# Narrow-head attention: steps of equal size, the first batch's split moved one phase ahead, one exponential for short units, loads and weights issued elsewhere

## What is computed

```python
x = x + _L0_attn_a(...)      # wide heads, not touched
x = x + _L0_ffn(...)         # experts, capacity routing
x = x + _L0_attn_b(...)      # narrow heads, cosine attention: |q| = |k| = 1, causal
x = x + _L0_ffn(...)
x = x + _L1_attn_a(...)      # narrow heads; query j of each 128 sees keys 0..j only
x = x + _L1_ffn(...)         # narrow heads, causal softmax; then 8 gated experts, top 2
x = x + _L1_attn_b(...)      # a recurrence (rwkv)
x = x + _L1_ffn(...)
# _L1_ffn, in short:
att = softmax(where(causal, q @ k.T / sqrt(8), -inf)); x = x + (att @ v) @ c_proj
h = gelu(x @ w1); y = h @ w2; x = x + sum of y of the two chosen experts, weighted
```

## Time and profile before

| | us |
|---|---|
| median of 3 runs | 2647.75 (2642.23 to 2649.84) |
| the profiled execution | 2645.61 |
| its span in the trace | 2643.7 |
| wide attention and first experts | 0 to 1051.6 |
| L0b: norms, attention | 1051.6 to 1071.6, 1072.3 to 1257.9 |
| window attention | 1435.8 to 1572.3 |
| L1 attention, first and second | 1600.4 to 1926.7, 2166 to 2493 |
| last gated experts | 2512.8 to 2643.7 |

### The profile page before, as it was taken

How to read it: one execution, slowest core, us unless ns; L and a number is a source line. 1 busy time by engine, 2 the same in 40 slices (tenths; PEclk the granted TensorE clock), 3 DMA queues, 4 the chain that set the end, 5 groups by cost and what they waited for, 6 DMA issues and landing times. The chain is left out here.

```text
span 2643.7 us, 37155 instructions
## 1 busy us (share of the span) xinstructions
PE 2140.0 (81%) x13716; PEld 1247.5 (47%) x13716; DVE 1591.2 (60%) x3477; ACT 1447.9 (55%) x2122; POOL 784.5 (30%) x428
## 2 busy tenths in 40 slices
PE   4999999999999538488346785999879737999798
PEld 3666666666666316122315342344347423444357
DVE  5978787787785465211564555777433666777324
ACT  3777777777777432598423243556653343555541
POOL 3877777687786002322003003000000031000000
PEclk7999999999999759699568796899989866999899
DMA  2000000000000310520501202211010012110010
GB/s 71 1 5 1 3 5 1 3 4 1 3 1 1 121 43 1 141 59 17 163 0 41 70 23 61 61 38 38 2 32 1 1 36 68 38 38 20 1 32 17
DMA packets 46411, 83.49 MB, mean 32 GB/s; under 512 B 11272, under 2 KB 19544, under 8 KB 43224
## 3 DMA queue, kind: packets, MB, share of 16 engines
q1 hardware_dynamic: 46232, 81.12, 11.2%
HBM read 64.09 MB, written 16.25 MB: 30 GB/s over the span
## 5 line engine op out<-in xcount | busy, mean ns | idle before, releaser
L713 ACT ACTIVATE probs<-psum_banks 128x1024 f32<-128x1024 f32 (+3 forms) x608 | 472.0, 827 | 357.3 <-PE psum_banks L581 258.6
L786 DVE TENSOR_REDUCE neg_max<-psum_banks 128x1 f32<-128x512 f32 (+3 forms) x672 | 398.5, 656 | 204.1 <-PE psum_banks L613 152.0
L1138 POOL TENSOR_SCALAR l0a_rows<-l0a_rows,l0a_rinv 128x1024 f32<-128x1024 f32 x160 | 454.4, 2845 | 188.8 <-DVE l0a_rinv L1100 185.1
L1088 DVE TENSOR_REDUCE l0a_nmax<-psum_banks 128x1 f32<-128x1024 f32 x256 | 312.4, 1220 | 137.7 <-PE psum_banks L982 135.7
L577 PE MATMUL psum_banks<-q_stack,k_stack 75*128 75x512 bf16 (+7 forms) x1216 | 295.6, 343 | 90.9 <-ACT probs L713 41.1
L1034 ACT ACTIVATE l0a_rows<-psum_banks,l0a_nmax 128x1024 f32<-128x1024 f32 x256 | 285.8, 1116 | 61.5 <-DVE l0a_nmax L1088 60.0
L609 PE MATMUL psum_banks<-k_stack,q_stack 72*128 72x128 bf16 (+3 forms) x1024 | 249.7, 327 | 79.3 <-DMA q_stack<-q_parts 67.2
L996 PE MATMUL psum_banks<-packed,l0a_rows 128*128 128x128 f32 x2048 | 266.2, 273 | 2.7 <-POOL l0a_rows L1138 1.6
L996 PEld LDWEIGHTS psum_banks<-packed,l0a_rows 128*128 128x128 f32 x2048 | 238.4, 141 | 42.9 <-issue 5.4
L981 PE MATMUL psum_banks<-l0a_kh,l0a_qw 128*128 128x512 f32 x512 | 241.1, 471 | 19.7 <-POOL l0a_qw L1127 13.5
L597 PE MATMUL psum_banks<-probs,v_ones 128*32 128x512 f32 (+3 forms) x2432 | 243.5, 515 | 7.7 <-ACT o_sum L682 6.5
(11 more groups left out here) (272 smaller groups left out, 3392.9 us busy)
## 6 DMA issues: line engine op xcount, KB each, us to landing
q_stack<-q_parts SPq DMA_DIRECT2D x72, 192.0 KB
k_stack<-k_parts SPq DMA_DIRECT2D x48, 192.0 KB
qkv<-in_l0f_w SPq DMA_DIRECT2D x6, 1024.0 KB, 5.5
q_parts<-parts SPq DMA_DIRECT2D x24, 256.0 KB, 3.3
k_parts<-parts SPq DMA_DIRECT2D x18, 256.0 KB, 4.9
moe_b<-in_l0f_b SPq DMA_DIRECT2D x32, 128.0 KB, 3.5
k_eight<-parts SPq DMA_DIRECT2D x16, 256.0 KB, 3.7
k_stack<-k_eight SPq DMA_DIRECT2D x16, 256.0 KB
```

What stands on the lines that cost most here:

```text
L713: act.activation(S.Pt[:, U % PBUFS, 2 * half:2 * half + 2, c0:HALF], PS[:, bank:bank + 2, c0:HALF], ACT.Exp).then_inc(exp_done, 1)
L786: dve.tensor_reduce(out, scores, AX, ALU.max, negate=True).then_inc(job_read, 1)
L1088: dve.tensor_reduce(R.nmax4[:, s % 4:s % 4 + 1], scores(s), AX, ALU.max, negate=True).then_inc(max_done, 1)
L1138: rows_divided.mark(pool.tensor_scalar(R.Pr[:, s % RING, :], R.Pr[:, s % RING, :], R.rinv4[:, s % 4:s % 4 + 1], None, ALU.mult))
```

## The change

It does six things. `narrow` (L0b only): a unit of at most 256 queries does all four heads in one visit of two banks with one exponential instead of two; `visits` counts them. The first batch item's split moves out of the attention phase: for L0b into the norm phase, for the others into the `passage` ahead (`split=`), with its stores, and that phase ends when they have landed; in the window only the 128 keys used are split and stored (`short_keys`). In L0b the second item's split moves from ACT and POOL to DVE. `side_jobs` has new tables. K and Q are loaded by one transfer each with a source read three times, and the c of a whole group by one transfer instead of four; loads are issued in another order. The gated experts' weights are loaded in the passage ahead.

```diff
+                for dst, at in loads:
+                    sp.dma_start(dst, at).then_inc(landed, 16)
+                for i in range(3 if split else 0):
+                    for n, w in enumerate((T, keys)):
+                        sp.wait_ge(part_done, max(part_no[g, n, i] for g in range(2) if (g, n) in widths))
+                        for home in homes(S, 0, n, i, keys, True):
+                            sp.dma_start(home.rearrange("d h t -> h d t"), parts[:, n, i, 0:w]).then_inc(stored, 16)
+                if loads:
+                    sp.wait_ge(landed, 16 * len(loads))
+                if split:
+                    sp.wait_ge(stored, 16 * 6)
...
+                                u, m = units[per * k + n], per * k + n
+                                act.wait_ge(post_ready, m + 1)
+                                act.activation(part(k, n, 0), PS[:, 4 + m % 4, 0:widths[k, n]], ACT.Copy,
+                                               scale=u.scale if u.scale is not None else 1.0).then_inc(part_done, 1)
...
+                    if divmod(n, per) in widths:
+                        dve.wait_ge(part_done, part_no[n // per, n % per, 0])
+                        dve.scalar_tensor_tensor(rest(*divmod(n, per)), bank[:, 0:widths[divmod(n, per)]],
+                                                 u.scale if u.scale is not None else 1.0, part(*divmod(n, per), 0), ALU.mult,
+                                                 ALU.subtract).then_inc(dve_read, 1)
...
+def short_keys(S, b, keys):
+    return S.k_parts[b, :, :, 0:NH * keys].rearrange("d j (h t) -> d j h t", t=keys)
...
             whole = ("turn", g, (0, 1))
-            if g >= lead:
-                s0 = 1 + (g - lead) * nu
-                late = 3 if g == lead and second else 0
-                spread(jobs, s0 + late, max(1, nu - (3 if second else 2) - late))
-                steps[s0 + max(1, nu - 3)].append(whole)
+            s0 = 1 + (g - lead) * nu
+            if g >= lead and not second:
+                spread(jobs, s0, nu)
+                steps[s0 + nu].append(whole)
+            elif g >= lead:
+                late = 2 if g == lead else -3
+                spread(jobs, s0 + late, nu - 3 - late)
+                steps[s0 + nu - 3].append(whole)
             elif second:
-                steps[0] += jobs[:len(first)] + [("turn", g, (0,))]
-                spread(jobs[len(first):], 1, 3)
+                rest = jobs[len(first):]
+                steps[0] += jobs[:len(first)] + rest[:3] + [("turn", g, (0,))] + rest[3:9]
+                spread(rest[9:], 1, 2)
                 steps[3].append(("turn", g, (1,)))
...
+            elif g == 0:
+                steps[0] += jobs
             else:
-                steps[0] += jobs + [whole]
+                steps[0] += jobs[:3] + [("turn", 0, (0, 1))] + jobs[3:]
+                steps[1].append(whole)
...
+    return steps[:1] + [sorted(events, key=lambda e: e[0] != "rows") for events in steps[1:]]
...
+    def narrow(U):
+        return not use_max and HALF - units[U % nu][2] <= HALF // 2
+    visits = [0]
+    for U in range(total):
+        visits.append(visits[-1] + (1 if narrow(U) else 2))
...
-                for copy in range(3 if use_max else 0):
-                    sp.dma_start(S.Kst[24 * copy:24 * (copy + 1), at, :],
-                                 S.k_parts[b, :, :, h0:h0 + 4, 0:keys].rearrange("d j h t -> (d j) h t")).then_inc(loaded[g % SLOTS], 16)
-                    sp.dma_start(S.Qst[copy:72:3, at, :],
-                                 S.q_parts[b, :, :, h0:h0 + 4, :].rearrange("j d h t -> (j d) h t")).then_inc(loaded[g % SLOTS], 16)
+                if use_max:
+                    k_rows = short_keys(S, b, keys)[:, :, h0:h0 + 4, :].rearrange("d j h t -> (d j) h t")
+                    q_rows = S.q_parts[b, :, :, h0:h0 + 4, :].rearrange("j d h t -> (j d) h t")
+                    sp.dma_start(S.Kst[0:72, at, :], k_rows.unsqueeze(0).to_broadcast([3, 24, 4, keys])).then_inc(loaded[g % SLOTS], 16)
+                    sp.dma_start(S.Qst[0:72, at, :], q_rows.unsqueeze(1).to_broadcast([24, 3, 4, T])).then_inc(loaded[g % SLOTS], 16)
...
-                for i in range(4):
-                    sp.dma_start(S.Qst[72:75, slot(g, i), HALF * sides[0]:HALF * (sides[-1] + 1)],
-                                 S.ct[w * i:w * (i + 1), k % 2, :]).then_inc(c_loaded[g % SLOTS], 16)
+                at, to = slice(slot(g, 0), slot(g, 3) + 1), slice(HALF * sides[0], HALF * (sides[-1] + 1))
+                if len(sides) == 2:
+                    sp.dma_start(S.Qst[72:75, at, to], S.ct[0:96, k % 2, :]).then_inc(c_loaded[g % SLOTS], 16)
+                for i in range(4 if len(sides) == 1 else 0):
+                    sp.dma_start(S.Qst[72:75, slot(g, i), to], S.ct[12 * i:12 * (i + 1), k % 2, :]).then_inc(c_loaded[g % SLOTS], 16)
...
+            load_group(0)
             if use_max:
                 for row in range(72, 75):
                     sp.dma_start(S.Kst[row:row + 1, :, :], S.ones_b[0:4 * SLOTS * keys // P, :]).then_inc(ones_set, 16)
...
-            store_batch(0)
-            for g in range(max(lead, 1)):
+            for g in range(1, SLOTS if lead == 2 else 1):
                 load_group(g)
             for e in turns:
                 if e[1] < lead:
                     load_c(e)
                     if e[2] == (0,):
                         load_group(lead)
-            for g in range(max(lead, 1) + sum(e[2] == (0,) for e in turns), SLOTS):
+            for g in range(SLOTS if lead == 2 else 1 + sum(e[2] == (0,) for e in turns), SLOTS):
                 load_group(g)
...
-            store_batch(1)
+            store_batch()
             for g in range(ng):
+                if lead == 2 and g + SLOTS < ng:
+                    load_group(g + SLOTS)
                 for e in turns:
                     if e[1] == g + lead and g + lead >= lead:
                         load_c(e)
-                if g + SLOTS < ng:
+                if lead < 2 and g + SLOTS < ng:
                     load_group(g + SLOTS)
...
-                for i in (2 * h, 2 * h + 1):
+                for i in range(2 * h, 4 if narrow(U) else 2 * h + 2):
                     bank = 2 * (n % pairs) + i % 2
-                    m = pe.matmul(PS[:, bank, c0:HALF], S.Kst[stack(i), slot(g, i), kt * P:(kt + 1) * P],
+                    to = slice(i // 2 * (HALF - c0), (i // 2 + 1) * (HALF - c0)) if narrow(U) else slice(c0, HALF)
+                    m = pe.matmul(PS[:, bank, to], S.Kst[stack(i), slot(g, i), kt * P:(kt + 1) * P],
...
-                if U in second_batch:
-                    parts(1, second_batch[U])
-                for half in range(2):
+                if use_max and U in second_batch:
+                    parts(second_batch[U])
+                for half in range(1 if U < total and narrow(U) else 2):
...
+                        if narrow(U):
+                            act.activation(S.Pt[:, U % PBUFS, :, c0:HALF].rearrange("p (h a) c -> p a h c", a=2),
+                                           PS[:, bank:bank + 2, 0:2 * (HALF - c0)].rearrange("p a (h c) -> p a h c", h=2),
+                                           ACT.Exp).then_inc(exp_done, 1)
+                            continue
...
-                if U in second_batch:
+                if use_max and U in second_batch:
                     i = second_batch[U]
-                    for n in (2, 3):
-                        pool.wait_ge(part_done, 6 + 2 * i + n % 2 + 1)
-                        if i < 2:
-                            x = chunks[n]
-                            pool.tensor_tensor(x, x, S.parts[:, n % 2, i, :], ALU.subtract).then_inc(rest_pool, 1)
...
+                if not use_max and s - 1 in second_batch:
+                    i = second_batch[s - 1]
+                    for n in range(2):
+                        part = S.parts[:, n, i, 0:part_width[n]]
+                        if i:
+                            dve.wait_ge(rest_done, 2 * (i - 1) + n + 1)
+                        dve.tensor_copy(part, chunks[n]).then_inc(part_done, 1)
+                        if i < 2:
+                            dve.wait_ge(part_done, 2 * i + n + 1)
+                            dve.tensor_tensor(chunks[n], chunks[n], part, ALU.subtract).then_inc(rest_done, 1)
...
+            chunks = [(QKt[:, i, NT * b:NT * (b + 1), :], (Q, K)[i][:, b * T:(b + 1) * T]) for b in range(B) for i in range(2)]
...
+                def _(sp):
+                    for n, i in part_order:
+                        sp.wait_ge(part_done, part_no[n, i])
+                        for home in homes(S, 0, n, i, T, False):
+                            sp.dma_start(home.rearrange("d h t -> h d t"), parts[:, n, i, :]).then_inc(stored, 16)
+                    sp.wait_ge(stored, 16 * 11)
...
-    moe_l0(S, D, channel_qkv(S, w["q"], w["k"], w["v"]))
+    moe_l0(S, D, channel_qkv(S, w["q"], w["k"], w["v"]), keys=P)
...
+                split=(parts, T))
...
```

(9 more changed lines are left out.)

181 lines of the change are left out of this document (114 added, 67 removed).

## The result

The changed kernel takes 2553.22 us, the median of 4 runs (2548.14 to 2556.03), against 2645.77 for the kernel before (4 runs, 2642.23 to 2649.84): a ratio of 0.9648, 95% interval 0.9625 to 0.9671. The forecast was 2569 with a range of 2529 to 2610.

A forecast was written before the change was run, and what follows sets the result against it. It took ACT to pace L0b, and DVE, PE and short chains to limit L1. From 2645.6 us, L0b -22, window -16, both L1 -32 and experts -7 summed to -77, giving 2569, range 2529 to 2610.

The forecast's parts named there:

- L0b, head: Start of L0b: the first item's split chain begins in the norm phase, so its load comes sooner; -4 us (0 to -7).
- Second item's split: L0b: moving the second item's split off ACT and POOL onto idle DVE saves 7 us (-4 to -9).
- Short units: L0b: merged short exponentials remove about two thirds of ACT's waiting for PE, 0.7 a side; -11 us (-5 to -16).
- Window: Window attention: sooner head -6, no wait for groups 2 and 3's rows -8, pace -2; -16 us (-8 to -26).
- K on three engines: Each L1: the single K load gets three engines; PE starts 4.3 us later, group 1's rows stall 6.5.
- L1, jobs moved: Each L1: nine side 1 jobs fill the wait for c and PE's bubble at the turn goes; -6 us (-3 to -9).
- L1, steady: Each L1: jobs spread over twelve steps, period 30.5 instead of 34; six times -3.5, -21 us (-8 to -28).
- Gated experts: Two gated expert stages: waits for weights shrink to about 1.5 us; twice -3.5, -7 us (-5 to -9).
- K on twelve engines: Rival for L1: the K load spreads over twelve engines all the same, -16 for each L1, 2537 us; chance 0.22.
- the hardly moving one: Rival for L1: PE's 31.72 is real work, so the period is 33, -1 instead of -3.5; 2599 us; chance 0.18.
- both loads on three engines: Rival for L1: Q's load also gets only three engines, period about 39, slower than before at 2700 us; chance 0.05.

The follow-up runs named there:

- e3: The changed kernel with two exponentials and two visits for every unit in L0b again, no merged ones: 2551.17 us in one run.
- e4: The changed kernel with the window's transfers reordered: groups 0 and 1, then the first c, then groups 2 and 3: 2556.48 us in one run.
- e7: The changed kernel with the window's eight row jobs of a group in one step again, instead of four in each of two: 2553.26 us in one run.
- e1: The changed kernel with K loaded by three transfers of 24 rows again, Q still by one: 2539.09 us.
- e9: The changed kernel with DVE's maxima of L1's full and tail jobs over 256 of 512 columns, leaving out work: 2533.82 us in one run.
- e2: The changed kernel with row jobs of groups 2 to 7 in L1 spread over the first 9 of 12 steps again: 2564.81 us.
- e5: The changed kernel with the gated experts' weights loaded and waited for in their own phase again: 2559.70 us.
- e11: The changed kernel as it is, profiled a second time: 2552.44 us.

## Why the prediction was right, point by point

The sign and the range held; the forecast gained 77 and the kernel 92.5. The window's gain was put too small; the short units' gain, the steady period's and the price of K on three engines too large; the clock's second fall was missing. By the table, whose spans differ by 90.3, the 13 us beyond the forecast are 11 in the window, 13 in L1 from the loads to the first sums and 5 in L1 from the first to the last sums, less 7 in L0b and 10 in the experts, with rests of about 2. So the total is near the forecast in part because large misses cancelled.

- *L0b, head* (-4): -2.6, within its bounds. (The 7.51 us of ACT that I took from the earlier trace rows for the six copies hold 1.3 us of a table load as well.) *Second item's split* (-7): e3 has it without the merged exponentials. Against before, its first side ends 2.0 us sooner after the first scores and the side of the next group 4.3 sooner after that: -6.3. Right.
- *Short units* (-11): -5.6 by e3, most of the shortfall in L0b. The failed step is "about two thirds of the waiting" would go; 0.16 to 0.25 of 0.92 went, and the side became 0.33 shorter, not 0.7. I read "ACT waits for PE" as missing banks; PE was busy with the values of the wider units.
- *Window* (-16): -27.1 from L0b's last sums to its own last (-7.5, -23.3, +3.7). The head gave 7.5 instead of 4, the first scores 5.1 instead of 2, and the failed term is "about 8 lie after that exponential": it was 17.9. I had priced one gap, the 8 us to the next row job, and not that the jobs pressed into single steps and the loads each delayed the steps behind it (e4, e7). The pace, which I had 0.4 shorter, is 0.17 longer, so the term of -2 came out as +3.7.
- *K on three engines* (+4.3 at PE's start, +6.5 later): the mechanism is shown, 3 records in the trace and 12 in e1. The size was off: the load took 13 us (1565.75 to 1578.77), not 18, for 24 + 6 rows an engine 0.43 a row and not 0.6. Once Q was done and only three engines worked it was 0.32: "with fewer engines at once" made each engine faster than I allowed. First row job: 5.1 later than before counted from the issue, where I had 9.7; the load itself was issued 5.8 sooner (-5.4 in the forecast), so that the first row job came 0.7 sooner instead of 4.3 later. The stall at group 1 was 1.46, not 6.5. The changed kernel left these 10 to 14 us on the table, which e1 takes back. The Trainium skill (*DMA: Bandwidth & Descriptors*, "Why a DMA increments its semaphore by 16 and not by 1" and "Rules for kernel authors") says that the number of engines must divide the slowest dimension of both sides, and that a leading broadcast with a stride of zero counts as one. By that rule the trace agrees: K, with three copies outermost, has 3 records, and Q, with 24 and 72, has 12.
- *L1, jobs moved* (-6): up to the first sums -1.9 with the stall of 1.46 in it, so -3.4 without; the first period, from group 0's side 0 to group 1's, went from 41.6 to 35.1, 4.0 more than a steady one. Together -7.4, within its bounds.
- *L1, steady* (-3.5 a period, six times: -21): a period gave 2.5, and only five of the seven are steady, -12.5. That the table has -22.6 and -24.5 beside -21 is luck: the first period's 4.0 beyond a steady one is in it, and the last period, from group 6 to group 7, is 3.2 and 6.0 shorter, which no term held and no run explains. The failed step is "Between 29 and 31.7 I take 30.5", which let PE's rows alone set the period. e9 puts them at 30.4 at most, near my figure, and DVE or the banks' chain adds 1. I had also put nearly all of the gain down to the spread; e2 shows 1.4 from it and 1.1 from the rest.
- *Gated experts* (-7): the waits went, -3.0 and -2.9. The price on the other side was missing: the clock's late rise and second fall, 4.7 and 4.3 in this execution, so the stages lost in it. e5 and e11 show that it comes and goes; in the medians the weights moved sooner are worth the forecast 7 (2559.70 less 2553.22 is 6.5).

Of the rivals, K on twelve engines (2537) looks like what e1 became, 2539, but the agreement is luck: twelve engines were worth 14, not the 32 it had, and the changed kernel was 16 below the forecast to begin with. The period of 31.5 lies between my 30.5 and the 33 of the hardly moving one; both loads on three engines was wrong by the 12 records of Q.

## What to carry to other kernels

Put the copies of a replicated load where they aren't the outermost dimension, or use one transfer for each copy: two transfers fewer to issue cost K a factor of four in engines, and three transfers of 24 rows were 10 to 14 us faster. When a wait for another engine is to be shortened, look at what that engine does in the wait before pricing it: PE was working. Small matmuls that stand in a run can be spread among large ones: the work is the same, and here the clock then stayed up. An engine's busy time is no proof that it sets the pace: PE's fell by 0.8 us a period when only DVE had less to do.

## What the runs showed of the hardware

- An 8 KB row took an engine 0.32 us while three engines worked by themselves (17 rows in 5.4 us), 0.43 over the whole load with K on three engines (24 + 6 rows in 13 us), and 0.7 when twelve were at it in the trace before (12 rows in 8.4 us).
- The granted clock fell from 1.00 to 0.50 (2.4 to 1.2 GHz) inside or 1.1 us behind a run of 32 small matmuls of 8 columns in which PE counts as fully busy, in some executions and not in others of the same kernel. It fell fully in all ten stages in which it had come up later than 5.1 us behind the first multiply; with these matmuls between 512-column ones it did not fall in four stages, three of them such late ones. A full fall took 6.8 us and cost some 3.3, the late rise about 1.
- DVE and POOL can slow one another, but not in every pair. In the start of L0b, DVE's first copy of the second item took 7.43 us beside POOL's memset and ended 0.55 us behind it; the two last such copies, with POOL idle, took 0.68. The memset took 6.92 us both here and in the trace before, where DVE's four subtractions beside it took 1.22 each. Four of POOL's masks took 5.09 us beside DVE's copies and subtractions, 1.1 to 1.6 each, where one takes 0.64 in the steady groups. What this cost the kernel no run shows; the first side still ended 3.1 us sooner after the first scores than before. POOL's timeline of the changed kernel, then DVE's:

```profile
1084.12 6.92 POOL L805 MEMSET v_ones<- 128x8192 f32 x1 [9.82 <-POOLq L69]
...
1095.32 5.09 POOL L822 TENSOR_SCALAR_AFFINE_SELECT probs<-probs 128x512 f32<-128x512 f32 x4
```

```profile
1084.16 7.43 DVE L854 CAST parts<-qkv 128x1024 bf16<-128x1024 f32 x1 [6.57 <-PEq L69]
```
